# One offset per block for three weight products: a sparse-expert loop with two register loads made one, its weights at a common stride, and five waits dropped on TensorE

## The reference, cut to what matters

```
scores = xt @ Wg.T                                  # xt: 8192 rows x 128
topk_scores, topk_idx = jax.lax.top_k(scores, 2)
gate = jax.nn.silu(jnp.einsum('td,ehd->teh', xt, W1))
up = jnp.einsum('td,ehd->teh', xt, W2)
y = jnp.einsum('teh,edh->ted', gate * up, W3)
w = jnp.einsum('tke,tk->te', onehot, topk_scores)
out = jnp.einsum('te,ted->td', w, y)
```

## Time and profile before

| | us |
|---|---|
| time, median of 3 runs | 3024.32 (3020.64 to 3024.77) |
| the profiled execution | 3028.85, its span 3027.0 |
| this stage's blocks, from the first transpose to the barrier behind the stage | from 1272 to 1611 |
| the loop of 13 turns (104 slots) in it | 1326.8 to 1579.4 |

### The profile page before, as it was taken

How to read it: one execution, slowest core, us unless ns; L and a number is a source line. 1 busy time by engine, 2 the same in 40 slices (tenths; PEclk the granted TensorE clock), 3 DMA queues, 4 the chain that set the end, 5 groups by cost and what they waited for, 6 DMA issues and landing times. The chain is left out here.

```text
span 3027.0 us, 82766 instructions
## 1 busy us (share of the span) xinstructions
PE 2734.3 (90%) x27846; PEld 2311.3 (76%) x27847; DVE 2098.6 (69%) x4560; ACT 1911.7 (63%) x4300; POOL 1944.2 (64%) x3245
## 2 busy tenths in 40 slices
PE   7999987999999999499997999995899999999996
PEld 6788766888888888388885888873677777777775
DVE  4777655677666666345555999997777878878543
ACT  3666544666666666255553777774778777777762
POOL 4566534556666666426667999985677777867652
PEclk9999998999999999699997999995899999999998
DMA  8566530000000000222222000000000000000000
GB/s 234 179 190 190 168 104 20 2 10 14 12 12 14 11 14 14 74 69 82 82 82 56 1 0 0 0 0 1 2 2 8 5 9 5 5 8 5 8 5 11
DMA packets 204792, 129.08 MB, mean 43 GB/s; under 512 B 13840, under 2 KB 197112, under 8 KB 203896
## 3 DMA queue, kind: packets, MB, share of 16 engines
q1 hardware_dynamic: 196344, 108.80, 12.1%
q0 software_dynamic: 8192, 16.79, 1.9%
HBM read 35.05 MB, written 90.51 MB: 41 GB/s over the span
## 5 line engine op out<-in xcount | busy, mean ns | idle before, releaser
L1558 PE MATMUL a_ps_s<-a_qk,w_ident 128*128 128x256 f32 x1024 | 239.1, 387 | 19.5 <-POOL a_qk L1665 18.4
L1013 POOL TENSOR_TENSOR x_p<-x_p,x_rz 128x1232 f32<-128x1232 f32 x64 | 143.9, 2248 | 170.0 <-DVE x_rz L1122 169.0
L635 DVE TENSOR_REDUCE a_nmax<-a_ps_s 128x4 f32<-128x512 f32 x256 | 164.9, 686 | 113.5 <-PE a_ps_s L381 109.9
L1665 POOL TENSOR_TENSOR a_qk<-a_qkv 128x2048 f32<-128x2048 f32 x64 | 235.5, 3680 | 2.6 <-POOL a_eight L218 1.0
L479 ACT ACTIVATE a_e<-a_ps_s 128x512 f32<-128x512 f32 x256 | 138.9, 595 | 151.2 <-PE a_ps_s L386 151.2
L1558 PEld LDWEIGHTS a_ps_s<-a_qk,w_ident 128*128 128x128 f32 x1024 | 192.3, 193 | 49.9 <-POOL a_qk L1665 22.1
L2384 POOL TENSOR_TENSOR x_sq<-x_e 128x1232 f32<-128x1232 f32 x64 | 143.2, 2237 | 125.2 <-DVE x_t_sq L2543 125.0
L1639 ACT ACTIVATE a_r<-a_o,w_a_rows 128x128 f32<-128x128 f32 x512 | 220.6, 521 | 2.4 <-DVE a_o L1724 1.7
L1393 POOL DMA_INDIRECT f_yg<-f_rows_out,f_index x120 | 115.1, 959 | 154.3 <-DVE f_yo L1473 137.9
L895 ACT ACTIVATE x_uu_hi<-x_ps_u 128x308 fp32r<-128x308 f32 x256 | 101.9, 423 | 111.5 <-PE x_ps_u L758 111.2
L1129 DVE TENSOR_REDUCE x_top<-x_ps_s 128x16 f32<-128x1232 f32 x64 | 91.2, 1424 | 114.4 <-PE x_ps_s L758 114.4
(11 more groups left out here) (627 smaller groups left out, 9648.2 us busy)
## 6 DMA issues: line engine op xcount, KB each, us to landing
f_rows_in<-a_zeros SPq DMA_DIRECT2D x31, 1088.0 KB, 5.4
f_rows_out<-a_zeros SPq DMA_DIRECT2D x31, 1088.0 KB, 8.8
f_xin<-f_rows_in SPq DMA_DIRECT2D x135, 64.0 KB
f_rows_out<-f_yo SPq DMA_DIRECT2D x135, 64.0 KB, 1.6
out<-x SPq DMA_DIRECT2D x16, 256.0 KB, 2.3
f_raw<-in_late_f SPq DMA_DIRECT2D x2, 1408.0 KB, 6.3
w_ctx<-in_ctx SPq DMA_DIRECT2D x1, 2464.0 KB
f_rows_in<-f_xr,f_where POOLq DMA_INDIRECT x128, 2.3
```

Of the source, the lines that this page charges most:

```text
L635: nc.vector.tensor_reduce(nmax[:, u % 2, g, :], ps_s[g][:, :].rearrange("p (t k) -> p t k", t=GROUP), AX.X, ALU.max, negate=True).then_inc ...
L1013: nc.gpsimd.tensor_tensor(wide, wide, rz[:, :].unsqueeze(2).broadcast_to([P, HEADS, K]), ALU.mult).then_inc(p_ready, 1)
L1558: ins = nc.tensor.matmul(ps_s[u % 2][:, 0:HEADS * HEADS], c.ident[:, :], qk[:, u % 2, k, :, :], start=k == 0, stop=k == HD - 1)
L1665: nc.gpsimd.tensor_tensor(qk[:, u % 2, :, :, :], qkv[:, u % UNROLL, 0, :, :].unsqueeze(3).broadcast_to(full), qkv[:, u % UNROLL, 1, :, :]. ...
```

## The change

Four edits, all in `sparse_experts`:

1. The gate and up weights are laid out at a stride of 384 columns per expert, like the down weights. One table, `at_expert` (number times 384), takes the place of `at_up` and `at_down`; the splits of the weights on ACT and DVE write with that stride, and DVE makes one small table less.
2. PE fetches the expert's offset once per block, and keeps it in a register (`held`) from the slot of its up products to that of its down product, three slots later. A register can't be kept from one turn of the loop to the next, so slots k = 0, 1 and 2 fetch the offset for the down product again.
3. The up products move from the head of slot t to the end of slot t-1 (`AHEAD = UP - 1`); on PE's own order of products this changes nothing. Their fetch stands at the head of the slot, ahead of the down product, which is behind the up products of the slot before. It was between the transposes and the up products.
4. In the loop PE no longer waits for five semaphores that other waits imply: `hi_ready`, `sg_ready` and `act_ready` before the up products, `lo_ready` before the transpose of x, `aT_ready` before those of the activations. In the straight slots `hi_ready` alone is dropped.

```diff
-        w_hi = [sb(f"w{n}_hi", [D, E * H], F32R) for n in range(2)]
-        w_lo = [sb(f"w{n}_lo", [D, E * H], F32R) for n in range(2)]
+        w_hi = [sb(f"w{n}_hi", [D, E * WIDTH], F32R) for n in range(2)]
+        w_lo = [sb(f"w{n}_lo", [D, E * WIDTH], F32R) for n in range(2)]
...
+            held = {}
+            def expert_of(b, name, lag):
+                if (name, lag) in held:
+                    return held.pop((name, lag))
+                return nc.values_load(at_expert[0:1, bass.ds(b, 1)], engines=[pe.engine], min_val=0, max_val=(E - 1) * WIDTH,
...
             def slot(t, k, i):
-                if (b := block_of(t, i, UP)) is not None:
-                    u = (k - UP) % 2
-                    up = nc.values_load(at_up[0:1, bass.ds(b, 1)], engines=[pe.engine], min_val=0, max_val=(E - 1) * H,
...
-                    pe.wait_ge(hi_ready, b + 1)
-                    pe.wait_ge(lo_ready, b + 1)
-                    for w, bank, taken, ready in ((0, ps_g, sg_ready, g_ps), (1, ps_u, act_ready, u_ps)):
-                        wait(pe, taken, b - 1)
...
+                name = "loop" if i is not None else t - k
+                if (b := block_of(t, i, AHEAD)) is not None:
+                    up = expert_of(b, "up", None)
+                    held[name, k - AHEAD] = up
                 if (b := block_of(t, i, DOWN)) is not None:
                     u = (k - DOWN) % 2
-                    down = nc.values_load(at_down[0:1, bass.ds(b, 1)], engines=[pe.engine], min_val=0, max_val=(E - 1) * 3 * D,
...
+                    down = expert_of(b, name, k - DOWN)
                     pe.wait_ge(aT_ready, b + 1)
                     wait(pe, y_ready, b)
...
-                    wait(pe, lo_ready, b - 1)
+                    if i is None:
+                        wait(pe, lo_ready, b - 1)
...
                     pe.wait_ge(act_ready, b + 1)
-                    wait(pe, aT_ready, b)
+                    if i is None:
+                        wait(pe, aT_ready, b)
...
+                if (b := block_of(t, i, AHEAD)) is not None:
+                    u = (k - AHEAD) % 2
+                    pe.wait_ge(lo_ready, b + 1)
+                    for w, bank, taken, ready in ((0, ps_g, sg_ready, g_ps), (1, ps_u, act_ready, u_ps)):
+                        if i is None:
+                            wait(pe, taken, b - 1)
...
-            nc.vector.tensor_scalar(at_up[:, :], ps_list[0:1, 2 * P:2 * P + ALL], float(H), None, ALU.mult)
-            nc.vector.tensor_scalar(at_down[:, :], ps_list[0:1, 2 * P:2 * P + ALL], float(3 * D), None, ALU.mult).then_inc(listed, 1)
+            nc.vector.tensor_scalar(at_expert[:, :], ps_list[0:1, 2 * P:2 * P + ALL], float(WIDTH), None, ALU.mult).then_inc(listed, 1)
```

More of the change, by code:

```diff
@@ L1196, in sparse_experts @@
     E, H = EXPERTS, 352
+    WIDTH = 3 * D
     EACH = 4
@@ L1219, in sparse_experts @@
         value = sb("value", [P, 2, 2])
-        at_row, at_up, at_down = (sb(n, [1, ALL], mybir.dt.int32) for n in ("at_row", "at_up", "at_down"))
+        at_row, at_expert = (sb(n, [1, ALL], mybir.dt.int32) for n in ("at_row", "at_expert"))
         xin = sb("xin", [P, 4, D])
@@ L1244, in sparse_experts, with each @@
         UP, TURN, DOWN = 2, 3, 4
+        AHEAD = UP - 1
         xr, yr = c.f0_x, c.f0_y
         last_row = (REGION * E + SPARE - 1) * P
+        def each(t, width):
+            return t[:, :].rearrange("p (e h) -> p e h", h=width)[:, :, 0:H]
         def done_by(j):
@@ L1310, in _ @@
             pe.wait_ge(w3_in, 16)
-            def slot(t, k, i):
-                if (b := block_of(t, i, UP)) is not None:
-                    u = (k - UP) % 2
-                    up = nc.values_load(at_up[0:1, bass.ds(b, 1)], engines=[pe.engine], min_val=0, max_val=(E - 1) * H,
-                                        skip_runtime_bounds_check_because="the expert's number is 0 to 7 before it is scaled")
-                    pe.wait_ge(hi_ready, b + 1)
-                    pe.wait_ge(lo_ready, b + 1)
-                    for w, bank, taken, ready in ((0, ps_g, sg_ready, g_ps), (1, ps_u, act_ready, u_ps)):
-                        wait(pe, taken, b - 1)
[L1321 to L1324, removed]
+            held = {}
[3 more added lines that the diff above has]
+                return nc.values_load(at_expert[0:1, bass.ds(b, 1)], engines=[pe.engine], min_val=0, max_val=(E - 1) * WIDTH,
+                                      skip_runtime_bounds_check_because="the expert's number is 0 to 7 before it is scaled")
+            def slot(t, k, i):
+                name = "loop" if i is not None else t - k
+                if (b := block_of(t, i, AHEAD)) is not None:
+                    up = expert_of(b, "up", None)
+                    held[name, k - AHEAD] = up
                 if (b := block_of(t, i, DOWN)) is not None:
                     u = (k - DOWN) % 2
-                    down = nc.values_load(at_down[0:1, bass.ds(b, 1)], engines=[pe.engine], min_val=0, max_val=(E - 1) * 3 * D,
-                                          skip_runtime_bounds_check_because="the expert's number is 0 to 7 before it is scaled")
+                    down = expert_of(b, name, k - DOWN)
                     pe.wait_ge(aT_ready, b + 1)
@@ L1345, in slot @@
                     ins.then_inc(aT_ps, 1)
+                if (b := block_of(t, i, AHEAD)) is not None:
[4 more added lines that the diff above has]
+                            wait(pe, taken, b - 1)
+                        out = bank[u][:, 0:H]
+                        nc.tensor.matmul(out, x_hi[:, u, :], w_hi[w][:, bass.ds(up, H)], start=True, stop=False)
+                        nc.tensor.matmul(out, x_hi[:, u, :], w_lo[w][:, bass.ds(up, H)], start=False, stop=False)
+                        nc.tensor.matmul(out, x_lo[:, u, :], w_hi[w][:, bass.ds(up, H)], start=False, stop=True).then_inc(ready, 1)
             run_blocks(pe, slot)
@@ L1353, in _ @@
                     act.wait_ge(raw_in, 16)
-                nc.scalar.activation(w_hi[n][:, :], raw[n][:, :], ACT.Copy).then_inc(split_hi, 1)
+                nc.scalar.activation(each(w_hi[n], WIDTH), each(raw[n], H), ACT.Copy).then_inc(split_hi, 1)
             act.wait_ge(padded, 1)
@@ L1447, in _ @@
             nc.vector.tensor_scalar(at_row[:, :], ps_list[0:1, 0:ALL], float(P), None, ALU.mult)
-            nc.vector.tensor_scalar(at_up[:, :], ps_list[0:1, 2 * P:2 * P + ALL], float(H), None, ALU.mult)
-            nc.vector.tensor_scalar(at_down[:, :], ps_list[0:1, 2 * P:2 * P + ALL], float(3 * D), None, ALU.mult).then_inc(listed, 1)
+            nc.vector.tensor_scalar(at_expert[:, :], ps_list[0:1, 2 * P:2 * P + ALL], float(WIDTH), None, ALU.mult).then_inc(listed, 1)
             for n in range(2):
                 dve.wait_ge(split_hi, n + 1)
-                nc.vector.tensor_tensor(w_lo[n][:, :], raw[n][:, :], w_hi[n][:, :].bitcast(F32), ALU.subtract).then_inc(split_lo, 1)
+                nc.vector.tensor_tensor(each(w_lo[n], WIDTH), each(raw[n], H), each(w_hi[n], WIDTH).bitcast(F32), ALU.subtract).then_inc(split_lo, 1)
             dve.wait_ge(padded, 1)
```

## The result

The kernel after takes 3000.5 us (median of five runs, 2999.02 to 3008.22). The kernel before took 3024.77 beside it (five runs, 3020.64 to 3029.09). The ratio is 0.9922, 95% interval 0.9904 to 0.9941, so 18 to 29 us less. The forecast was 3005.0, range 2993 to 3017.

The account below looks back on a forecast made before the run. PE's sequencer was taken as the bound, with two rings through other engines next. 15.4 + 4.2 + 2.0 - 2.5 = 19.1 us off the median 3024.3 gave 3005.2, range 2993 to 3017.

Parts of the forecast that it names:

- The bound: In the loop PE's sequencer, at 2.37 us a slot, sets the pace; the array needs about 2.07 and waits.
- No change: Rival, 13%: the array, not the sequencer, sets the pace, so fetches are hidden anyway; 0 to 4 us less, about 3023.
- The prices of sequencer instructions: On PE's sequencer a short instruction costs 0.126 us, a table load about 0.3; a turn falls from 19.4 to 14.4.
- Ring A: POOL's gather, DVE's combine and copy, SP's store and load, PE's transpose: turn shrinks 1.40 to 18.0; 15.4 us over 11 turns.
- Ring B: Input block's transpose to the load two blocks later and its landing: 17.3 us a turn, binding two turns, 4.2 us gained.
- The straight slots: The 39 slots outside the loop lose one load and one wait each: 2 us gained, between 0 and 3.9.
- The splits: DVE's two strided weight splits before the loop run over as many elements: 0, between -0.3 and +0.6 us.
- The late blocks: Input blocks landing late in the loop no longer find slack to absorb them: three such, an estimate, cost 2.5 us.
- Slower by late landings: Rival, 4%: a faster loop packs DMA closer and blocks land late; up to 35 us slower, 3059.
- L: Time for an input block's load to land after its issue: taken as 1.9 us, between 1.6 and 2.38.
- The price of a `tensor_load`: PE's table load costs about 0.3 us by the trace, against the skill's floor of about 600 ns.

Follow-up runs that it names:

- before_store_later: The kernel before, with only SP's store of the finished rows one slot later, behind the next input load; turn 19.34 us, ratio 0.9979.
- waits_only_loose: The kernel before without the five waits in the loop, with SP's store one slot and DVE's combine two slots later; turn 17.44 us.
- load_only_loose: The kernel after with the five waits put back, SP's store one slot later and DVE's combine two slots later; turn 18.13 us.
- both_later: The kernel after with SP's store one slot later and DVE's combine two slots later; 2992.67 us, ratio 0.9875, turn 17.23 us.
- store_later: The kernel after with only SP's store of a block's result one slot later; 2993.23 us, ratio 0.9902.
- combine_later: The kernel after with only DVE's combine of the gathered rows two slots later; 3003.79 us, ratio 0.9913.
- down_later: both_later with the down product one slot later, its result's copy first on DVE, PE's activation wait at the next transposes; 3033.32 us, ratio 0.9931.

## Why the prediction was right, and where its sizes were off

- **The bound: right.** It said that PE's sequencer set the pace and the array waited at the up products. `before_store_later` shows that the link through SP had slack, and `waits_only_loose` and `load_only_loose` that a shorter sequencer sum is what moves the turn. "No change" falls with it: 0 to 4 us less were its mark. The Trainium skill, Advanced Engine Details and Errata, Engine Queue Depths, gives TensorE's queue as 64 deep, and the rival took it that such a queue hides the fetches. In these traces it did not: slots with a second fetch last 2.33 to 2.47 beside 2.09, with the sequencer's own sum at 2.37.
- **The prices of sequencer instructions: right, but one detail of their sum was wrong.** 2.37 us for a slot with a second load and the waits was met by 2.47 and 2.33, and half a microsecond for the loop's turn by 0.43. But the text summed the sequencer over a turn (14.4 us) and set 16.6 for PE alone, as if the loop's turn were hidden. It is not in `both_later`, so PE's floor is 17.23. That raises the floor by 0.6 and didn't show, since rings bound first.
- **Ring A: 18.0 a turn forecast, 17.8 measured.** The last 11 turns took 195.3 us in place of 212.6, 17.3 less where 15.4 were forecast. The gather's wait came up by name, as forecast. Its last link was told wrong: not only SP's store and load, but PE's own wait for the copy closes it, and loosening the first alone (`store_later`) left the turn at 17.78. That 18.0 came so near is in part luck: ring B alone would have held the turn at 17.9.
- **Ring B: undersized.** Forecast 17.3, as the limit of the first two turns alone. By itself it gives 17.9 (`combine_later`), nearly as much as ring A. The first two turns lost 3.6 us (39.9 to 36.4), not 4.2. What the sum lacked stands at the loop's turn, where it added 0.5 us: that slot lasts 2.84 there, beside 2.0 to 2.2 for the others. A possible reason, not tested by itself, is that a sequencer that was held by a block has no lead there: the idle time before the down product is 0.72 us in the timeline after and 0.46 in `both_later`. The wait for the block was to show by name on PE; in the window shown it doesn't, since each single one is under 0.1 us.
- **The straight slots: 2.8 us, forecast 2.0**, within the bounds of 0 to 3.9. **The splits: 0**, as forecast.
- **The late blocks: the step that failed.** 2.5 us were charged for three late blocks that spent slack would no longer absorb. Turns of the loop in which a block came late were there before too (20.61 and 19.64 us where 19.35 is usual; the kernel after has one of 18.64 where 17.77 is). In the straight slots each has one such block, 3.1 us from issue to landing before and 3.2 after. So the two profiles pay about alike. It is the largest error of the sum: without it the forecast is 21.6 for this stage, and 23.7 was measured. The rest is ring A's 1.9 and the straight slots' 0.8, less ring B's 0.6.
- **Slower by late landings: did not come.** Ring B passes 19.4 only at a landing of 2.4 us; in slots 32 to 119 of the kernel after those that bound took 1.8 to 2.0. Single blocks took 2.9 to 3.2 in `combine_later`, and cost single turns.
- **The range.** Its lower end for L = 1.6, 3002, counts ring A alone. The prediction's own ring B would add 1.4 us or more in the first two turns, so about 3001. The range itself, down to 2993, is not touched by it.
- **The price of a `tensor_load`.** The Trainium skill, DMA: Bandwidth & Descriptors, Latency and other measured facts, puts its floor at about 600 ns. The rows after show 298 to 308 ns, about as before, and the measurement decides.

## What to carry to other kernels

When an engine reads nearly full, look for "issue" ahead of one line and add up its sequencer's instructions for one round: here 0.126 us for each wait or register step and 0.30 for a table load; five waits a slot that others implied cost nearly 2 us a turn of eight slots, once the rings were loose. Sum it slot by slot: in these kernels a slot whose sequencer needed more than the array was not made good by the next. Before forecasting a gain, walk every ring (a cycle of waits that leads from the engine through others back to it), and follow each to all its ends; where two rings are equally long, loosening one shows nothing, so try both together before giving either up.

## What the runs showed of the hardware that was not expected

- The array's own pace in this mix is steady to a few ns: in the straight slots of `both_later` slot after slot of 2.086 to 2.089 us, 16.70 for eight.
- A turn of the loop costs PE 0.43 us on the mean in `both_later`, and something near it in every turn (that slot lasts 2.49 to 2.55 us beside 2.09), with the array idle ahead of the down product.
- In `down_later` an issue of SP's showed 0.02 us while POOL was issuing gathers, and ACT and DVE stood still together for 2.55 us behind it. The cause was not found.
- Stages with unchanged code differ by some microseconds from one execution to the next (the last stage took 966.0 to 976.1 us in the traces of this case). A change of this size is read inside its own stage.
